# The last 22 down products of a routed feed-forward layer in three f16 products

## The reference

```
for e in range(8):
    gate = x @ ws[e, :512, :].T          # 256 -> 512
    up   = x @ ws[e, 512:, :].T
    h    = silu(gate) * up
    out += combine[:, e:e+1] * (h @ w2s[e].T)   # 512 -> 256, the down product
```

## Time and profile before

| | us |
|---|---|
| median of 3 runs | 526.11 |
| lowest, highest | 524.04, 527.46 |
| the profiled execution, its own time | 523.54 |
| its span, first to last instruction | 521.4 |

### The profile page before, as it was taken

The page is one execution under the profiler, slowest core; times in us unless marked ns, Lnnn a source line. Parts: engine busy times, 40 slices in busy tenths (PEclk is TensorE's granted clock), DMA queues, the critical chain, the costliest instruction groups (busy, mean ns, idle before and its releaser), DMA issues.

```text
span 521.4 us, 9268 instructions
## 1 busy us (share of the span) xinstructions
PE 441.9 (85%) x2920; PEld 269.4 (52%) x2920; DVE 309.5 (59%) x1108; ACT 273.4 (52%) x386; POOL 226.7 (43%) x314
## 2 busy tenths in 40 slices
PE   2999589899987899889936899999999999999900
PEld 0555224445553555445513567666667666666600
DVE  6275998877779887987697334465323332232224
ACT  0476349998867668665938334532333323323215
POOL 0000021112675567655844376554555655655322
PEclk9999759999999999989977799999999999999965
DMA  8378899222146324422320114343323333233164
GB/s 278 59 207 246 259 379 369 76 64 78 55 131 203 122 62 111 134 61 83 127 76 11 30 31 92 51 89 54 57 49 61 52 53 62 44 58 52 21 158 185
DMA packets 32976, 57.23 MB, mean 110 GB/s; under 512 B 5025, under 2 KB 23585, under 8 KB 31394
## 3 DMA queue, kind: packets, MB, share of 16 engines
q1 hardware_dynamic: 18306, 39.60, 23.8%
q0 software_dynamic: 7488, 10.27, 12.3%
q10 hardware_dynamic: 7136, 6.77, 4.3%
HBM read 38.64 MB, written 17.97 MB: 109 GB/s over the span
## 4 chain that ended last, share of the span: by engine, by line
PE 58%; DVE 23%; ACT 9%; DMA 4%; issue 4%; SPq 1%; ACTq 0%; DVEq 0%; POOLq 0%
PE PS L1371 20%; PE PS L1398 12%; DVE PS L877 8%; PE PS L1207 5%; PE PS L1168 4%; PE PS L1390 3%; PE PS L1242 3%; PE PS L1189 2%; DVE B L981 2%; ACT PT L724 2%; PE PS L416 2%; PE PS L1363 2%; DMA qk_parts<-W 2%; PE PS L1261 1%; DMA sum_rows<-PT,IDXA 1%
## 5 line engine op out<-in xcount | busy, mean ns | idle before, releaser
L877 DVE CUSTOM_DVE_ANT_0 PS<-PS,CB 128x512 f32<-128x512 f32 (+3 forms) x256 | 120.4, 514 | 29.8 <-PE PS L1168 28.7
L1371 PE MATMUL PS<-W,PT 128*128 x468 | 114.9, 382 | 1.9 <-ACT PT L826 1.6
L724 ACT ACTIVATE PT<-PS 128x1024 f32<-128x1024 f32 x80 | 81.3, 1022 | 36.3 <-PE PS L1190 35.7
L683 POOL DMA_INDIRECT sum_rows<-PT,IDXA x39 | 62.0, 1591 | 70.3 <-ACT PT L837 65.1
L1168 PE MATMUL PS<-KQ 96*128 96x512 bf16 (+3 forms) x256 | 66.9, 327 | 19.7 <-DVE MX L877 14.1
L1126 DVE SCALAR_TENSOR_TENSOR PT<-PS,CW,PT 128x512 f32<-128x512 f32 x39 | 29.3, 750 | 68.1 <-ACT PT L830 68.1
L1371 PEld LDWEIGHTS PS<-W,PT 128*128 128x128 f16 x468 | 44.4, 98 | 41.0 <-issue 4.0
L1189 PE MATMUL PS<-KQ 104*128 104x512 bf16 (+3 forms) x256 | 61.0, 310 | 1.1 <-ACT PT L724 1.1
L1132 DVE COPY PT<-PS 128x512 f32<-128x512 f32 x39 | 27.0, 691 | 52.3 <-PE PS L1390 52.3
L826 ACT ACTIVATE PT<-PS 128x512 f16<-128x512 f16 x39 | 23.3, 597 | 63.2 <-PE PS L1363 63.2
L837 ACT ACTIVATE PT<-PS,WS 128x256 f32<-128x256 f32 x39 | 18.5, 474 | 72.0 <-PE PS L1398 72.0
(11 more groups left out here) (183 smaller groups left out, 740.9 us busy)
## 6 DMA issues: line engine op xcount, KB each, us to landing
W<-w1T SPq DMA_DIRECT2D x8, 1024.0 KB, 14.5
qk_parts<-W SPq DMA_DIRECT2D x32, 192.0 KB, 3.1
KQ<-qk_parts SPq DMA_DIRECT2D x32, 192.0 KB, 2.9
KQ<-qk_parts SPq DMA_DIRECT2D x64, 64.0 KB, 2.8
x_rows<-X1S ACTq DMA_DIRECT2D x4, 516.0 KB, 3.5
W<-xT SPq DMA_DIRECT2D x4, 512.0 KB, 6.8
KQ<-qk_parts SPq DMA_DIRECT2D x16, 128.0 KB, 2.9
sum_rows<-X ACTq DMA_DIRECT2D x4, 512.0 KB, 3.1
```

Source lines behind the costliest of these rows:

```text
L683: pool.indirect_dma_start(acc_dram, bass.IndirectOffsetOnAxis(ap=IDXA[:, j, 0:1], axis=0), YS[j % TRIO], None, compute_op=ALU.add).then_in ...
L724: act.activation(PT[n][:, :], STb[slot_of(k, n)].rearrange("p a n -> p (a n)"), ACT.Exp).then_inc(s["exp"], 1)
L877: last = dve.tensor_tensor_reduce(src, src, maskS[:, TT * P - w:], 1.0, LOW, ALU.add, ALU.max, MX[p][:, h, i:i + 1])
L1371: last = mm(dst, XGT[j % TRIO][:, x_part, k, :], w1h[:, bass.ds(at, UNIT)], start=(k == x_part == w_part == 0), stop=(k == KC - 1 and x_pa ...
```

## The change

Tiles 0 to 16 keep their form. For tiles 17 to 38 (SPLIT_FROM = 17):

- `hidden(j)` on VectorE computes HH as before, then the largest absolute value of each token's 512 hidden values (HM), that times 2^-14 (HB), its reciprocal (RI), and the token's result weight times HB (WS2). `hidden_high` on ScalarE writes HH x RI as f16 (HHI), `hidden_low` on VectorE the remainder as f16 (HLO).
- `split_hidden_T` makes eight f16 transposes in place of four f32 ones, the high part into bank HP, the low part into bank 5; ScalarE copies the first out (`hidden_columns`), VectorE the second.
- `split_down` makes twelve f16 products of 256 columns in place of four f32 ones, and follows two steps behind its tile in place of one.
- The W2 weights are split before: squares in steps 1 to 4 (two per step, 1024 columns each), their sum by a small product and two VectorE operations in step 5, powers on GpSimd in step 6 (`down_scales`), high parts on ScalarE in steps 7 to 14, low parts on VectorE in steps 9 to 16, two units of 512 per step each. The parts lie in buffers that attention has left.
- The last stage's statistics lie in O in place of K[3]. A memset of SQ2 and the buffers are added.

The core of the diff:

```diff
+            def down_scales():
+                pool.wait_ge(s["f22"], 1)
+                pool.tensor_tensor(ROOT2[0][:, :], F22[1][:, :], MHALF[:, :], ALU.pow)
+                pool.tensor_tensor(ROOT2[1][:, :], F22[1][:, :], HALF[:, :], ALU.pow).then_inc(s["root2"], 1)
...
+                if j == 5 + 1:
+                    down_scales()
...
+            def down_squares(c):
+                act.wait_ge(s["sq2"], c + 1)
+                act.activation(JUNK, W2[c // 2][:, c % 2 * 1024:c % 2 * 1024 + 1024], ACT.Square,
+                               accum_out=SQ2[:, c:c + 1]).then_inc(s["sq2"], 1)
+            def down_high(u):
+                act.wait_ge(s["sc2"], 2)
+                act.activation(W2H[u // 4][:, u % 4 * 512:u % 4 * 512 + 512], W2[u // 4][:, u % 4 * 512:u % 4 * 512 + 512], ACT.Copy,
+                               scale=SW2[:, :]).then_inc(s["hi2"], 1)
+            def hidden_high(j):
+                i = j - SPLIT_FROM
+                act.wait_ge(f["ri"], i + 1)
+                act.activation(HHI, HH, ACT.Copy, scale=RI[:, i:i + 1]).then_inc(f["hhi"], 1)
+            def hidden_columns(j):
+                act.wait_ge(f["th2"], j - SPLIT_FROM + 1)
+                act.wait_ge(f["yp"], j)
+                act.activation(HTH[:, 0, :, :].rearrange("p k t -> p (k t)"), HPh[0], ACT.Copy).then_inc(f["hta"], 1)
...
+                if 1 <= j < 1 + N2 // 4:
+                    for c in range(2 * (j - 1), 2 * (j - 1) + 2):
+                        down_squares(c)
+                if 7 <= j < 7 + N2 // 2:
+                    for u in range(2 * (j - 7), 2 * (j - 7) + 2):
+                        down_high(u)
+            for j in range(SPLIT_FROM, NTILES):
+                act.wait_ge(f["h"], j)
+                silu(j)
+                if j == SPLIT_FROM:
+                    result(j - 1)
+                elif j >= SPLIT_FROM + 2:
+                    split_result(j - 2)
+                if j + 1 < NTILES:
+                    columns(j + 1)
+                if j > SPLIT_FROM:
+                    hidden_columns(j - 1)
+                hidden_high(j)
...
+            def down_low(u):
+                at = slice(u % 4 * 512, u % 4 * 512 + 512)
+                dve.wait_ge(s["hi2"], u + 1)
+                dve.scalar_tensor_tensor(W2L[u // 4][:, at], W2[u // 4][:, at], SW2[:, :], W2H[u // 4][:, at],
+                                         ALU.mult, ALU.subtract).then_inc(s["lo2"], 1)
+            def hidden(j):
+                i = j - SPLIT_FROM
+                combine_weight(j)
+                dve.wait_ge(f["sil"], j + 1)
+                dve.wait_ge(f["u"], j + 1)
+                if i == 0:
+                    dve.wait_ge(f["th"], SPLIT_FROM)
+                else:
+                    dve.wait_ge(f["hlo"], i)
+                dve.scalar_tensor_tensor(HH, U, CW[:, :], SIL, ALU.mult, ALU.mult).then_inc(f["h"], 1)
+                dve.wait_ge(f["h"], j + 1)
+                link(dve.tensor_reduce(HM[:, i:i + 1], HH, AX.X, ALU.max, apply_absolute_value=True))
+                link(dve.tensor_scalar(HB[:, i:i + 1], HM[:, i:i + 1], 1e-30, HSCALE, ALU.max, ALU.mult))
+                dve.reciprocal(RI[:, i:i + 1], HB[:, i:i + 1]).then_inc(f["ri"], 1)
+                dve.wait_ge(f["ws"], j + 1)
+                dve.scalar_tensor_tensor(WS2[:, i:i + 1], WS[:, j:j + 1], HB[:, i:i + 1], CC[:, :], ALU.mult, ALU.mult).then_inc(f["ws2"], 1)
+            def hidden_low(j):
+                i = j - SPLIT_FROM
+                dve.wait_ge(f["hhi"], i + 1)
+                dve.scalar_tensor_tensor(HLO, HH, RI[:, i:i + 1], HHI, ALU.mult, ALU.subtract).then_inc(f["hlo"], 1)
+            def hidden_columns(j):
+                dve.wait_ge(f["th2"], j - SPLIT_FROM + 1)
+                dve.wait_ge(f["yp"], j)
+                dve.tensor_copy(HTH[:, 1, :, :].rearrange("p k t -> p (k t)"), HPh[1]).then_inc(f["htd"], 1)
...
+                if 9 <= j < 9 + N2 // 2:
+                    for u in range(2 * (j - 9), 2 * (j - 9) + 2):
+                        down_low(u)
+            dve.wait_ge(s["sc2"], 2)
+            for j in range(SPLIT_FROM, NTILES):
+                hidden(j)
+                if j > SPLIT_FROM:
+                    hidden_columns(j - 1)
+                hidden_low(j)
+            hidden_columns(NTILES - 1)
...
+            def split_hidden_T(j):
+                i = j - SPLIT_FROM
+                if i:
+                    pe.wait_ge(f["hta"], i)
+                    pe.wait_ge(f["htd"], i)
+                else:
+                    pe.wait_ge(f["ht"], SPLIT_FROM)
+                pe.wait_ge(f["hhi"], i + 1)
+                pe.wait_ge(f["hlo"], i + 1)
+                for r, part in enumerate((HHI, HLO)):
+                    for k in range(FF // P):
+                        last = nc.tensor.transpose(HPh[r][:, k * P:(k + 1) * P], part[:, k * P:(k + 1) * P], IDH[:, :])
+                last.then_inc(f["th2"], 1)
+            def split_down(j, e):
+                i = j - SPLIT_FROM
+                pe.wait_ge(f["hta"], i + 1)
+                pe.wait_ge(f["htd"], i + 1)
+                pe.wait_ge(f["ys"], j)
...
+                for k in range(FF // P):
+                    for h_part, w_part in ((0, W2H), (0, W2L), (1, W2H)):
+                        last = mm(YP[:, 0:E], HTH[:, h_part, k, :], w_part[k][:, bass.ds(e * E, E)],
+                                  start=(k == 0 and h_part == 0 and w_part is W2H), stop=(k == FF // P - 1 and h_part == 1))
+                last.then_inc(f["yp"], 1)
...
+                if j == 5:
+                    pe.wait_ge(s["xt"], B * 2)
+                    pe.wait_ge(s["sq2"], N2 // 2 + 1)
+                    mm(TB[1][:, 0:N2 // 2], ONESF[:, :], SQ2[:, :], start=True, stop=True).then_inc(s["sqp2"], 1)
                 hidden_T(j)
                 e_before = e
-            down(NTILES - 1, e_before)
+            experts = [None, e_before]
+            for j in range(SPLIT_FROM, NTILES):
+                if j == NEARLY:
+                    pe.wait_ge(s["tab"], 2)
+                e = expert(j)
+                gate(j, e)
+                if j == SPLIT_FROM:
+                    down(j - 1, experts[1])
+                elif j >= SPLIT_FROM + 2:
+                    split_down(j - 2, experts[0])
+                if j + 1 < NTILES:
+                    rows_T(j + 1)
+                up(j, e)
+                if j > SPLIT_FROM:
+                    split_hidden_T(j - 1)
+                experts = [experts[1], e]
+            split_down(NTILES - 2, experts[0])
+            split_hidden_T(NTILES - 1)
+            split_down(NTILES - 1, experts[1])
```

More of the change, by code:

```diff
@@ L68 @@
 SPARE = 2 * UNIT
+SPLIT_FROM = 17
+NSPLIT = NTILES - SPLIT_FROM
+HSCALE = 2.0 ** -14
+N2 = FF // P * NX * E // 512
 NSG, NTG = 10, 5
@@ L122, in block_kernel @@
         WLO = sb("WLO", [P, UNIT])
+        SQ2 = sb("SQ2", [P, N2 // 2])
+        F22 = [sb(f"F22{n}", [P, 1]) for n in range(2)]
+        ROOT2 = [sb(f"ROOT2{n}", [P, 1]) for n in range(2)]
+        SW2 = sb("SW2", [P, 1])
+        CC = sb("CC", [P, 1])
+        HM, HB, RI, WS2 = (sb(n, [P, NSPLIT]) for n in ("HM", "HB", "RI", "WS2"))
         F2 = [sb(f"F2{n}", [P, 1]) for n in range(2)]
@@ L197, in block_kernel @@
         YS = [PT[4][:, 256 * n:256 * n + 256] for n in range(3)]
+        JUNK = PT[0][:, :]
+        HHI, HLO = (PT[0][:, 256 * n:256 * n + 256].bitcast(F16) for n in range(2))
+        HTH = PT[0][:, 512:1024].bitcast(F16).rearrange("p (r k t) -> p r k t", r=2, k=FF // P)
+        W2H = [VR[:, :, :].rearrange("p n f -> p (n f)")[:, 1024 * k:1024 * k + 1024].bitcast(F16) for k in range(FF // P)]
+        W2L = [v.rearrange("p h t -> p (h t)").bitcast(F16) for v in (K[2], Q[2], K[3])]
+        W2L += [AO[:, :, :].rearrange("p n f -> p (n f)").bitcast(F16)]
         IDXA = sb("IDXA", [P, NTILES, 1 + TOPK], I32)
@@ L235, in block_kernel @@
                  "mt", "at", "atc", "ap", "res", "x1", "xb", "tp", "xt", "lgp", "lg", "mc", "rkp", "rk", "mrun", "dve", "dl", "ex",
-                 "ab", "tm", "tacc", "dec", "cp", "cnt", "var", "rs", "wts", "tab", "xh", "xl", "sq", "sqp", "f2", "root", "sc", "hi", "lo", "lop")
+                 "ab", "tm", "tacc", "dec", "cp", "cnt", "var", "rs", "wts", "tab", "xh", "xl", "sq", "sqp", "f2", "root", "sc", "hi", "lo", "lop",
+                 "sq2", "sqp2", "f22", "root2", "sc2", "hi2", "lo2")
         s = {n: sem("b_" + n) for n in names}
@@ L240, in block_kernel @@
         s_xb, s_x1w, s_rows, s_w = sem("s_xb"), sem("s_x1w"), sem("s_rows"), sem("s_w")
-        f = {n: sem("c_" + n) for n in ("xt", "xgt", "g", "u", "sil", "h", "th", "ht", "yp", "ys", "ws")}
+        f = {n: sem("c_" + n) for n in ("xt", "xgt", "g", "u", "sil", "h", "th", "ht", "yp", "ys", "ws", "ri", "hhi", "hlo", "ws2", "th2", "hta", "htd")}
         s_g = [sem(f"s_xg{q}") for q in range(TRIO)]
@@ L246, in block_kernel @@
         XPh = XP.bitcast(F16)
+        HPh = [b.bitcast(F16)[:, 0:FF] for b in (HP, bank[5])]
         def nth(j):
```

(36 more changed lines are left out.)

10 lines of the change are left out of this document (9 added, 1 removed).

## The result

The changed kernel takes 541.37 us in the median of 4 runs (540.52 to 544.55), beside 525.36 for the kernel before in the runs of the same comparison (4 runs). The ratio is 1.0312, with a 95% interval from 1.0256 to 1.0368: slower by 3%. The profiled execution took 540.52 us, with a span of 538.7; before it was 523.54 and 521.4.

The account below looks back on a forecast made before the run. TensorE was taken to bound the kernel at 4.98 us a tile. Late stage +18.3 and early splitting +1.7 make +20.0 us: 543.5 on the profiled execution, 546.1 on the median, so 545 us; range 536 to 554.

Parts of the forecast that it names:

- a ring that closes through VectorE's order: Late tiles: HH, scaling, copy, down, row transposes, up, next HH; 5.75 us a round in place of 4.98.
- the likeliest case: Whole kernel: late tiles 5.75 us apart with the f16 copy at 0.69 us; 545 us, chance 0.52.
- rival A: VectorE's f16 copy from PSUM streams twice as fast, 21 x 0.27 = 5.7 us less: 539 us, chance 0.31.
- the end: After the last HH: the result of tile 37 is out after 4.65 us, before 2.14; 2.5 us more.
- The copy of 512 f16 values out of PSUM: VectorE's copy of the low columns in late tiles: taken as 0.69 us from the f32 copy, 0.42 if twice as fast.
- From tile 17 on: HH of tile 17 to HH of tile 38: 3.65 plus 20 rounds of 5.75, where 21 x 4.98 = 104.6 stood.
- early work: Splitting the down weights in the early tiles: squares, high and low parts, small product; +1.7 us.
- The step-11 term: Two low parts in step 11, where VectorE has no idle time before HH: +1.2 us after 0.3 of room.
- the squares and their small product: Early steps: two squares a step in tiles 1 to 4, +0.4 us; small product for their sum, +0.1.
- Rival B: Late tiles: TensorE stays the bound, 22 x 0.43 = 9.5 us gained, 1.7 + 0.9 lost: 518 us, chance 0.05.
- Rival C: Early tiles: table loads at the squares; chance 0.07, its size is not in the text given.
- Rival D: Late tiles: idle gaps of 1.2 us a round let TensorE's clock fall: 551 us, chance 0.05.

Follow-up runs that it names:

- The first experiment: Changed kernel with VectorE's copy of the low columns of tile j-1 moved right behind HH, ahead of the maximum: 522.94 us, ratio 0.995 to the kernel before.

## Why the prediction was right or wrong

The direction and its cause were right: slower, by a ring that closes through VectorE's order. 545 us stands beside 541.37 measured; the result lies in the range. But the likeliest case was not the one that came. What came is rival A, the f16 copy at the faster rate, with its chance of 0.31. On its own base the forecast was 543.5 and the profiled execution took 540.52. That it came so near is in part luck: the copy was 5.7 us too long in the sum, while the rest of the ring and the end were 3.4 too short.

The terms of the ring, as predicted and as measured (449.08 to 454.69):

| term | predicted | measured |
|---|---|---|
| HH with its link | 0.78 | 0.79 |
| maximum with its link | 0.71 | 0.72 |
| scale, to the reciprocal | 0.19 | 0.18 |
| reciprocal to weight, weight to copy | 0.18 | 0.20 |
| the copy | 0.69 | 0.42 |
| copy's end to the down product | 0.14 | 0.20 |
| down, row transposes, up | 2.97 | 3.00 |
| to the next HH | 0.09 | 0.10 |
| sum | 5.75 | 5.61 |

- **The term that was mis-sized** is "The copy of 512 f16 values out of PSUM": 0.69 was taken from the f32 copy as the nearest row, and 0.42, the lower bound, was the value. The argument for it, that PSUM's port sets the pace, since the product L1126 and the copy L1132 differ little, fell: the doubled copy shows 0.68 with an f32 output and 0.41 with an f16 one from the same PSUM columns. Two f32 rows can't tell what 16 bits do. 21 copies at 0.27 are 5.7 us too much. The Trainium skill ("VectorE: DVE Perf Modes", section "The perf-mode tier table") allows a copy from PSUM up to twice the basic rate, and the same page (section "What auto-detection actually checks") asks that every tensor be 16 bits wide for the packed rate; this case agrees with both, 0.42 and 0.68. A rule of the Trainium skill that speaks of exactly the new operation deserved more weight than a row of another format.
- **The rest of the ring** was 0.13 too short, 2.6 us over 20 rounds. Half of that is the 0.20 from the copy to the down product; the 0.14 had been read at an f32 product. Why it is longer was not tried. The other terms were each within 0.03. TensorE idle ahead of the down product was to be 1.2 us and is 0.86: a tile takes 1.03 over TensorE's own 4.57, and the other 0.17 lies in the down product itself, whose piece of the chain is 1.48 behind the gap and 1.31 without one.
- **From tile 17 on** the trace has 11.1 us for 14.1 predicted (118.65 against 104.6); that is the copy less the rest.
- **Up to tile 17** it has 3.34 us for 3.43 (early work 1.7, the old down product ahead of the up product 1.73). The splitting alone cost 1.68 by the trace. The step-11 term, +1.2, measured 1.3 to 1.4 by what moving it gave. The remaining 0.3 stands for the squares and their small product (0.5 predicted): HH of tile 4 comes 1.85 us late against before, and tile 5 makes all but 0.3 of it good.
- **The end** has 3.3 us for 2.5. The term itself was right: the scatter of tile 37 starts 4.78 after the last HH where it was 2.42, 2.4 more. What the sum left out is that the last two scatters start 5.07 apart where they stood 4.41 apart, and 0.3 in the read-back. In the chain the first of the two lands after 4.03 us (3.67 before). In the other runs the distance lay between 4.8 and 6.2; why a landing takes longer was not tried.
- **Rival B** (TensorE stays the bound) had the right condition and too low a time. Its condition was that VectorE's stretch from HH to the copy's end be under 1.35 us. The first experiment makes it 1.08 by order alone (442.35 + 0.41 - 441.68), and the tiles run at 4.57 us, where 4.55 was worked out. The 518 us were too low by 4 to 5. By the trace 2.2 of this is the end (3.1 us longer than before, for 0.9), and 1.7 is the old down product ahead of up(17), which the forecast counts and B's sum doesn't.
- **Rival C** (table loads at the squares) fell by the loads in the profile (its own terms also add up to 10, not 9). **Rival D** (a lower clock) fell by the clock of 1.00 in the stage.

The expected gain on TensorE, 0.43 us a tile, is there: its work fell to 4.57 us. It was not seen in the time since another ring of 5.61 took the place of the 4.98, and the gain appears once the copy stands right behind HH. Little of it reaches the total even then: of the 8.8 us gained between HH of tile 17 and of tile 38, 3.4 go to the stretch up to tile 17 and 3.1 to the end.

## What to carry to other kernels

When a change lengthens what lies between two products, write down the closed ring from an instruction of one tile to the same instruction of the next, through every engine's program order, and compare it with the busiest engine's work; an operation that nobody waits for belongs behind the one that somebody does. With a tile on the bound of one engine, look at the next serial chain too (here the scatters, 4.4 to 4.7 us apart), before the gain is written down. For a price that no row shows, find or make a row of the same format, not only of the same size.

## What the runs showed of the hardware that was not expected

- VectorE's copy of 128x512 from PSUM takes 0.42 us from f16 to f16, 0.68 from f16 to f32, and 0.69 from f32 to f32. An f16 source alone isn't enough; f32 to f16 was not run.
- TensorE stood idle for 0.86 us in each of 5.6, and its granted clock was 1.00 (2.4 GHz) in every stretch from 400 to 500 us.
- A gap of TensorE was put down to "issue" although an instruction of another engine released it; moving that instruction made it vanish. The kind of product doesn't decide this: at the last down product of the kernel before, whose W2 columns a register selects as well, the profile names VectorE's copy (L1132, 0.87 us).
